# Attention of a four-stage kernel: two heads in one 32-row PSUM tile, earlier row turns, another order of the splits

## The reference

```python
q = q.reshape(B, S, H, DK); k = k.reshape(B, S, H, DK); v = v.reshape(B, S, H, DK)
scores = jnp.einsum('bqhd,bkhd->bhqk', q, k) / np.sqrt(DK)
attn = jax.nn.softmax(scores, axis=-1)
o = jnp.einsum('bhqk,bkhd->bqhd', attn, v).reshape(B, S, D)
x = x + o @ w_o + b_o            # layer 0; layer 1 multiplies by proj_w.T and adds proj_b
```

## Time and profile before

| what | value |
|---|---|
| median of 3 runs | 1201.21 us (1199.15 to 1223.79) |
| the profiled execution | 1201.9 us |
| its span | 1200.1 us |
| mean granted TensorE clock | 0.859 of 2.4 GHz |
| attention of layer 0, about | 92 to 359 us |
| attention of layer 1, about | 796 to 1031 us |
| PE, DVE, ACT, POOL busy | 70%, 69%, 51%, 39% of the span |

### The profile page before, as it was taken

One profiled execution on the slowest core, in us unless ns is written; L12 is line 12 of the kernel. 1 busy time (PEld: TensorE's weight loads), 2 busy tenths in 40 slices (PEclk: granted clock), 3 DMA queues, 4 the chain that ended last, 5 costly groups with the idle time before them and its releaser, 6 DMA issues. The chain is left out here.

```text
span 1200.1 us, 24485 instructions
## 1 busy us (share of the span) xinstructions
PE 839.7 (70%) x6994; PEld 483.7 (40%) x6994; DVE 824.7 (69%) x1748; ACT 610.8 (51%) x1269; POOL 465.8 (39%) x700
## 2 busy tenths in 40 slices
PE   2856888888862688878893444438999989567663
PEld 1631333333322466666682222213333333245443
DVE  5636888888828244555443688757888987399983
ACT  2752666666534155655462576616767777222221
POOL 3861233333330566767652344321111111155553
PEclk9985999999875699999897666758999999788896
DMA  6482222222100333433342143341212120000000
GB/s 208 141 272 76 61 63 63 63 63 63 50 14 1 99 120 106 126 107 118 114 124 76 52 140 108 117 143 47 65 55 67 55 67 28 1 10 9 17 18 17
DMA packets 111514, 94.28 MB, mean 79 GB/s; under 512 B 10671, under 2 KB 98506, under 8 KB 111328
## 3 DMA queue, kind: packets, MB, share of 16 engines
q1 hardware_dynamic: 105920, 83.31, 22.3%
q0 software_dynamic: 4608, 8.93, 2.5%
q10 hardware_dynamic: 928, 1.32, 0.3%
HBM read 59.18 MB, written 34.08 MB: 78 GB/s over the span
## 5 line engine op out<-in xcount | busy, mean ns | idle before, releaser
L973 DVE TENSOR_REDUCE neg_max<-bank 128x2 f32<-128x512 f32 x512 | 324.2, 684 | 55.0 <-PE bank L1083 54.5
L1063 ACT ACTIVATE pr<-score 128x512 f32<-128x512 f32 x512 | 280.0, 603 | 149.6 <-PE score L1140 147.5
L1140 PE MATMUL score<-qs,ks 51*128 51x256 bf16 x1024 | 177.7, 282 | 45.8 <-DMA qs<-max_rows 32.8
L1083 PE MATMUL bank<-ks,qs 48*128 48x256 bf16 x1024 | 182.5, 290 | 31.5 <-DMA qs<-q_scratch 30.8
L1158 PE MATMUL p_o<-pr,vs 128*9 128x256 f32 x2048 | 167.9, 395 | 0.4 <-ACT pr L1063 0.4
L1140 PEld LDWEIGHTS score<-qs,ks 51*128 51x128 bf16 x1024 | 68.0, 96 | 197.7 <-issue 72.2
L917 POOL TENSOR_TENSOR max_parts<-neg_max,one 128x16 bf16<-128x16 f32 x64 | 13.8, 216 | 266.0 <-DVE neg_max L973 266.0
L1322 POOL DMA_INDIRECT y_scratch<-y_all,to_i x72 | 76.6, 1064 | 67.0 <-DVE y_all L1428 57.6
L1316 POOL DMA_INDIRECT y_all<-hn_scratch,token_i x72 | 75.6, 1050 | 54.9 <-DVEq L1409 34.0
L1502 ACT ACTIVATE h_t<-p_t,vec 128x128 f32<-128x128 f32 x72 | 33.0, 458 | 120.6 <-PE p_t L1598 59.8
L1619 PE MATMUL p_y<-w,hid 128*128 x576 | 87.5, 297 | 0.1
(11 more groups left out here) (287 smaller groups left out, 1725.9 us busy)
## 6 DMA issues: line engine op xcount, KB each, us to landing
w_now<-w_dram SPq DMA_DIRECT2D x72, 256.0 KB
ks<-k_scratch SPq DMA_DIRECT2D x128, 96.0 KB, 2.2
qs<-q_scratch SPq DMA_DIRECT2D x128, 96.0 KB, 2.3
k_scratch<-parts SPq DMA_DIRECT2D x16, 384.0 KB, 2.6
q_scratch<-parts SPq DMA_DIRECT2D x16, 384.0 KB, 2.6
k_scratch<-parts SPq DMA_DIRECT2D x16, 256.0 KB, 2.2
q_scratch<-parts SPq DMA_DIRECT2D x16, 256.0 KB, 2.5
both<-y_scratch SPq DMA_DIRECT2D x8, 512.0 KB, 4.0
```

The lines of the kernel that those rows point to most:

```text
L973: dve.tensor_reduce(neg_max[:, i // HALF, :, col:col + 1], bk[:].rearrange("p (q t) -> p q t", t=L), AX.X, ALU.max, negate=True).then_inc( ...
L1063: act.activation(pr[s % N_PR][:, 2 * k:2 * k + 2, :], score[k][:], ACT.Exp, scale=SCALE).then_inc(exp_done, 1)
L1083: return pe.matmul(bk[:, qt * L:(qt + 1) * L], qs[u][rows, place(h), qt * P:(qt + 1) * P], ks[u][rows, place(h), :], start=True, stop=True)
L1140: scored = pe.matmul(score[k][:, j, :], ks[u][rows, place(h), kt * P:(kt + 1) * P], qs[u][rows, place(h), :], start=True, stop=True)
```

## The change

1. Two heads share a 32-row tile. The value operand `vs` has 18 columns for each head, 9 of them zero: heads of an even head group use columns 0 to 8, those of an odd group 9 to 17. The products of four steps (two head groups) are added up in the same PSUM rows. `p_o` has one 256-column region for each half of the heads. ScalarE moves 128 x 256 instead of 128 x 512, TensorE turns 4 blocks in all instead of 8, and one division (reciprocal of 128 x 32, product of 128 x 256) stands for two. The rows of the output weights are put in the new order on the host.
2. The uses: three "norm" uses (divide at step 2, turn at 3, project at 4) instead of four, and none at step 1; "rows" 0 goes ahead of the scores and maxima of step 5 instead of behind them.
3. GpSimd: `rows_ready(b - 2)` right after split half 1, instead of `rows_ready(b - 1)` after split half 0; `x_now`, `mv`, `ve` get two buffers for it; `copy_v` becomes two copies; two memsets of `vs` at the start of each attention. Its loop is written out. SP stores the rows of b - 2 behind the first of the two row transfers.
4. A sequence has 21 uses instead of 22, and TURN = 4 of them fill whole rounds of the banks: the middle 14 sequences are two written out and a loop over 3 x 4.

```diff
-        vs = [sb(f"vs{u}", [P, 2, H, VW]) for u in range(2)]
+        vs = [sb(f"vs{u}", [P, 2, H, 2 * VW]) for u in range(2)]
...
-        o_raw = sb("o_raw", [P, HG, L])
-        o_rec, o_n, o_t = sb("o_rec", [P, 2, H]), sb("o_n", [P, 2, H, DK]), sb("o_t", [P, L])
+        o_raw = sb("o_raw", [P, 2, L])
+        o_rec, o_n, o_t = sb("o_rec", [P, 2 * 2 * JT, 2]), sb("o_n", [P, 2 * 2 * JT, 2, DK]), sb("o_t", [P, L])
...
-        p_o = S.ps(ctx, "p_o", [P, HG, L])
+        p_o = S.ps(ctx, "p_o", [P, 2, 512])
...
-        AT = {1: [("rows", 1), ("norm", 0)], 2: [("norm", 1)], 3: [("norm", 2)], 4: [("norm", 3)], 5: [("rows", 0)]}
+        NORM = ("divide", "turn", "project")
+        AT = {1: [("rows", 1)], 2: [("norm", 0)], 3: [("norm", 1)], 4: [("norm", 2)]}
+        BEFORE = {5: [("rows", 0)]}
...
-            uses = [("max", head + 2), ("max", head)] + AT.get(s, [])
+            uses = BEFORE.get(s, []) + [("max", head + 2), ("max", head)] + AT.get(s, [])
...
-            if NB > 2:
-                with eng.Fori(0, (NB - 2) // 2) as pair:
-                    seq(pair * 2 + 1, 1, "middle")
-                    seq(pair * 2 + 2, 0, "middle")
-            seq(NB - 1, 1, "last")
+            ahead = (NB - 2) % TURN
+            for b in range(1, 1 + ahead):
+                seq(b, b % TURN, "middle")
+            with eng.Fori(0, (NB - 2) // TURN) as turn:
+                for b in range(1 + ahead, 1 + ahead + TURN):
+                    seq(turn * TURN + b, b % TURN, "middle")
+            seq(NB - 1, (NB - 1) % TURN, "last")
...
                 load(b + 2, u, 0)
                 maxima_to_queries(b + 1, 1 - u, 0, left(b, kind, ("rows", 0)))
+                if keeps:
+                    keep_rows(b - 2, u)
                 sp.wait_ge(score_full, (b + 1) * HALVES)
                 load(b + 2, u, 1)
                 maxima_to_queries(b + 1, 1 - u, 1, left(b + 1, "middle", ("rows", 1)))
-                if kind != "start":
-                    keep_rows(b - 1, 1 - u)
...
-                pool.tensor_copy(vs[u][:], S.v_all[:, bass.ds(2 * b, 2), :, :]).then_inc(v_copied, 1)
+                for a in range(2):
+                    held = vs[u][:].rearrange("p k (g a j) w -> p (k g) a j w", a=2, j=JT)[:, :, a, :, a * VW:(a + 1) * VW]
+                    whole = S.v_all[:, 2 * b:2 * b + 2, :, :].rearrange("p k (g a j) w -> p (k g) a j w", a=2, j=JT)
+                    copied = pool.tensor_copy(held, whole[:, :, a, :, :])
+                copied.then_inc(v_copied, 1)
...
+            for u in range(2):
+                pool.memset(vs[u][:], 0.0).then_inc(v_cleared, 1)
+            pool.wait_ge(v_cleared, 2)
...
-            if NB > 2:
-                with pool.Fori(0, (NB - 2) // 2) as pair:
-                    for u in range(2):
-                        b = pair * 2 + u + 1
-                        split(b, 1, left(b - 1, "middle", ("max", H - 3)))
-
-                        pool.wait_ge(pr_free, b * STEPS + N_PR)
-                        copy_v(b + 1, u)
-                        split(b + 1, 0, left(b, "middle", ("max", HALF - 3)))
-                        rows_ready(b - 1, u, pair)
+            for b in range(1, NB - 1):
+                split(b, 1, left(b - 1, "start" if b == 1 else "middle", ("max", H - 3)))
+                if b > 1:
+                    rows_ready(b - 2)
+
+                pool.wait_ge(pr_free, b * STEPS + N_PR)
+                copy_v(b + 1, (b + 1) % 2)
+                split(b + 1, 0, left(b, "middle", ("max", HALF - 3)))
...
-                    sn.turn((c * 2 + stage) * 1)
-                    heads = bk[:].rearrange("p (h r) -> p h r", r=32)
-                    sn.link(dve.reciprocal(o_rec[:, stage, :].unsqueeze(2), heads[:, :, DK:VW]))
-                    dve.tensor_tensor(o_n[:, stage], heads[:, :, 0:DK],
-                                      o_rec[:, stage, :].unsqueeze(2).broadcast_to([P, H, DK]), ALU.mult
-                                      ).then_inc(bank_free, 1)
...
+                    sn.turn(c)
+                    heads = bk[:].rearrange("p (t r) -> p t r", r=32)[:, :, 0:2 * VW].rearrange("p t (a w) -> p t a w", w=VW)
+                    sn.link(dve.reciprocal(o_rec[:], heads[:, :, :, DK]))
+                    dve.tensor_tensor(o_n[:], heads[:, :, :, 0:DK], o_rec[:].unsqueeze(3).broadcast_to([P, 2 * 2 * JT, 2, DK]),
+                                      ALU.mult).then_inc(bank_free, 1)
...
-                two = slice(2 * half, 2 * half + 2)
-                act.copy(o_raw[:, two, :], p_o[:, two, :]).then_inc(o_moved, 1)
...
+                act.copy(o_raw[:, half, :], p_o[:, half, 0:L]).then_inc(o_moved, 1)
...
-                    for hg in range(HG):
-                        last = pe.transpose(bk[:, hg * P:(hg + 1) * P], o_raw[:, hg, i * P:(i + 1) * P], S.ident)
...
+                    for qt in range(2):
+                        for half in range(2):
+                            at = (qt * 2 + half) * P
+                            last = pe.transpose(bk[:, at:at + P], o_raw[:, half, qt * P:(qt + 1) * P], S.ident)
...
-                    last = pe.matmul(p_o[32 * j:32 * j + VW, hg, :], vs[u][:, kt, hg * JT + j, :],
-                                     pr[s % N_PR][:, j, :], start=kt == 0, stop=kt == 1)
+                    last = pe.matmul(p_o[32 * j:32 * j + 2 * VW, hg // 2, 0:L], vs[u][:, kt, hg * JT + j, :],
+                                     pr[s % N_PR][:, j, :], start=s % (STEPS // 2) == 0,
+                                     stop=s % (STEPS // 2) == STEPS // 2 - 1)
```

More of the change, by code:

```diff
@@ L761, in phase_attention @@
         if layer == 0:
[L762 removed]
+            stats, rstd = sb("stats", [P, 2, 6]), sb("rstd", [P, 2])
+            mv, ve, x_now = ([sb(f"{n}{u}", [P] + shape) for u in range(2)]
+                             for n, shape in (("mv", [2, 2]), ("ve", [2]), ("x_now", [2, ROW])))
             hn = [sb(f"hn{u}", [P, 2, D]) for u in range(2)]
[L764 removed]
+            lg_raw = sb("lg_raw", [P, 2, E])
             stats_done, mv_done, var_ready, rstd_ready, hn_ready, lg_scaled = (
@@ L804, in base, with bank_of @@
             return 0 if kind == "first" else BASE0 if kind == "start" else BASE1 + (b - 1) * len(SEQ)
-        def bank_of(kind, u, i):
-            before = {"first": 0, "start": BASE0, "middle": BASE1 + (1 - u) * len(SEQ), "last": BASE1}[kind]
+        def bank_of(kind, v, i):
+            before = {"first": 0, "start": BASE0}.get(kind, BASE1 + (v - 1) % TURN * len(SEQ))
             return bank[(before + i) % N_BANK]
@@ L878, in follow @@
                 maxima_to_queries(b + 1, 1 - u, 1, left(b + 1, "middle", ("rows", 1)))
-                if kind != "start":
-                    keep_rows(b - 1, 1 - u)
             maxima_to_queries(0, 0, 0, left(0, "first", ("rows", 0)))
             maxima_to_queries(0, 0, 1, left(0, "start", ("rows", 1)))
[L884 to L888, removed]
-            follow(NB - 3, 1, "middle")
+            follow(0, 0, "start", False)
+            follow(1, 1, "middle", False)
+            with sp.Fori(0, (NB - 4) // 2) as pair:
+                follow(pair * 2 + 2, 0, "middle")
+                follow(pair * 2 + 3, 1, "middle")
             maxima_to_queries(NB - 1, 1, 0, left(NB - 2, "middle", ("rows", 0)))
-            keep_rows(NB - 3, 1)
+            keep_rows(NB - 4, 0)
             maxima_to_queries(NB - 1, 1, 1, left(NB - 1, "last", ("rows", 1)))
@@ L895, in _ @@
             if layer == 0:
+                keep_rows(NB - 3, 1)
                 keep_rows(NB - 2, 0)
@@ L1002, in norm @@
                         dve.wait_ge(hn_ready, c + 1)
-                        dve.tensor_tensor(x_now[:], S.rows[:, two, :], proj, ALU.add).then_inc(bank_free, 1)
+                        dve.tensor_tensor(x_now[u][:], S.rows[:, two, :], proj, ALU.add).then_inc(bank_free, 1)
                     else:
@@ L1006, in norm, with statistics @@
                                           ).then_inc(bank_free, 1)
-            def statistics(c, x_added):
+            def statistics(c, u, x_added):
                 dve.wait_ge(bank_free, x_added)
@@ L1012, in statistics, with variances @@
                 for n in range(2):
-                    last = dve.bn_stats(stats[:, n, :], x_now[:, n, 0:D])
+                    last = dve.bn_stats(stats[:, n, :], x_now[u][:, n, 0:D])
                 last.then_inc(stats_done, 1)
-            def variances(c):
+            def variances(c, u):
                 dve.wait_ge(stats_done, c + 1)
@@ L1037, in _ @@
             if layer == 0:
-                dve.sem_inc(hn_ready, 1)
+                dve.sem_inc(hn_ready, 2)
             for i, what in enumerate(FIRST):
-                consume(0, i, bank_of("first", 0, i), what)
+                consume(0, 0, i, bank_of("first", 0, i), what)
             sequences(dve, seq)
-            for stage in range(4):
+            for stage in range(len(NORM)):
                 i = len(LAST) + stage
```

(11 more changed lines are left out.)

93 lines of the change are left out of this document (50 added, 43 removed).

## The result

The changed kernel takes 1132.6 us (median of 4 runs, 1130.1 to 1135.9) beside 1201.7 before: a ratio of 0.943, 95% interval 0.940 to 0.947. The forecast was 1147 in a range of 1128 to 1174: direction and place were right, the gain was larger than forecast. The measured time is outside the 1140 to 1154 that the forecast itself covered.

The account below looks back on a forecast made before the run. VectorE was taken as nearly the bound, made to wait by in-order TensorE. Savings of 31.9 us (layer 0), 18.3 (layer 1) and 4.4 (edges), together 54.6 from 1201.9, gave 1147 us, range 1128 to 1174.

Parts of the forecast that it names:

- Step 1 and the transfer of half 1: Layer 1: step 2 starts 0.58 us earlier, but step 4 waits for half 1's rows until 6.2, losing 0.25.
- Rows 0 before step 5: Layer 1: SP starts half 0 about 0.85 us behind step 5 instead of 1.96; rows land at 11.9.
- The rest of layer 1: Step 5 to next step 0: sequence reaches 11.9 us, plus 0.2 for queueing, taken as 12.1 instead of 13.41.
- Layer 0: Middle sequences: VectorE floor 12.4 us, the 1.0 us split wait gone; 12.7 us taken instead of 14.98.
- Weight load: Value products: 9 more columns cost 0 to 8 ns a load, 0 to 0.5 us a sequence; taken as 0.
- The loop of four: Loop body of four sequences may not stay held on the chip: 0 to 60 us; taken as 0.
- The clock: Both layers: clock falls come where TensorE's two 1 us stalls lie together; none expected after, inside 14.98 - 12.7.
- the edges: First and last sequences and tails: 0.6, 0.7 and 0.9 us saved, each twice, 4.4 us together.
- VectorE at its floor with no queueing: Rival, both layers: sequences of 12.4 and 11.5 us, gain 67, so 1135 us; chance 0.17.
- The half gain through a new wait: Rival: single division or GpSimd's split at step 5 holds TensorE 0.5 us in 28 sequences, 1161 us; chance 0.23.
- the transfers exchanged: Rival: layer 1's transfer wait merely becomes half 1's, layer 0 gains only the split's wait, 1170 us; chance 0.11.
- the slower side: Rival: 18-column value products lose side-by-side running (1237 us at 0.35 a step), or the loop stalls each turn; chance 0.04.

Follow-up runs that it names:

- e3: Changed kernel with only rows 0 back behind the scores and maxima of step 5; 1131.2 us, 0.967 of the kernel before.
- e4: Changed kernel with only rows_ready back behind split half 0, now of sequence b - 1; 1135.5 us, 0.970 of the kernel before.
- e10: Changed kernel with the turn back at step 4 and the output-weight product at step 5, each one step later; 1146.9 us, 0.944 of the kernel before.
- e8: Changed kernel with the division done as two reciprocals and two products again, on the one bank; 1105.2 us, 0.937 of the kernel before.
- e5: Changed kernel with one more, unread VectorE copy of 128 x 256 in each sequence; 1099.7 us, 0.933 of the kernel before.
- e11: Changed kernel with the copy of the turned block on ScalarE and a one-column memset on VectorE instead; 1132.6 us, 0.932 of the kernel before.
- e6: Kernel before the change with one more, unread VectorE copy of 128 x 256 in each sequence; 1181.4 us, ratio 1.002.
- e1: Changed kernel with the old order of rows and splits, so only the packing is left; 1152.4 us, 0.986 of the kernel before.

## Why the prediction was right, and where its sizes were off

**What bounds the kernel.** Right: TensorE's two waits on the path of the maxima. e3 and e4 brought them back one at a time.

**Step 1 and the transfer of half 1.** The forecast was step 4 at 6.2 from zero, where the rows land, and so "late next". It came at 6.18, in a profile that lists no wait for it. That a gap of 0.07 us decides there showed only when e10 took the other path away.

**Rows 0 before step 5.** Right in kind: SP 0.71 us behind the step for 0.85 forecast, the wait gone, worth 0.75 and 1.21 us (e3). GpSimd's thin cover held; no wait for it at step 5.

**The rest of layer 1.** The chain gave 11.9, and 11.80 was measured. The step that was off is "I add 0.2 for queueing between the two and take 12.1": nothing came on top of the chain. 14 x 0.27 = 3.8 us.

**Layer 0.** The same: I took 12.7 over a floor of 12.4 and it came to 12.28, 14 x 0.42 = 5.9 us. The floor itself was too high. Busy time counts each instruction to the end of its record, and where VectorE runs without a break the next one starts some 0.08 us before that end (a reduction lasts 0.68 and the next follows after 0.60). Where TensorE was late before the change, this overlap was missing, and the time looked like work. The sum of starts, 12.31, is the right one. The split's wait left 0.3 us each of its 1.0.

**VectorE's division.** Forecast 0.64 from start to start; it is 865.93 - 865.20 = 0.73, because the reciprocal of 32 takes 342 ns and not about 300. Undone (e8) it is worth 7 us: it was priced as VectorE's work, but in layer 1 it counts through the turn that waits for it.

**ScalarE's move.** 378 ns for a forecast of 400.

**Weight load.** 96 ns instead of 89, so 7 ns for 9 columns, near the upper bound of 8; the nearest row, by which I took 0, was misleading. It is hidden all the same: the score follows the value products by 0.56 us (862.98 to 863.54), as the 0.56 of before in the earlier trace rows (937.01 to 937.57). The Trainium skill's rule on loads ("TensorE: Matmul & The Clock Gate", section "LDWEIGHTS (loading the stationary operand)") gave 7.5 ns for the difference, by an estimate, and the trace agrees for these two. The 13 us that it would have cost unhidden didn't come.

**The loop of four.** At nothing, and right for TensorE. The whole run has 40 instruction packets on one queue for 30 before. From 205 to 282 us, which takes in the loop's turn at about 243 us, the changed kernel shows none of them and one on the other queue:

```profile
q8 instruction: 40, 0.66, 0.2%
```

```profile
q1 hardware_dynamic: 12808, 6.05, 27.0%
q14 instruction: 1, 0.01, 0.0%
```

No packet comes on the first queue from 193 to 205 us either, where the loop turns for the first time. So the turns bring no burst of packets, and the body of four seems to be held as well. The Trainium skill's page "Runtime: NRT & Kernel Launch" (section "Instruction fetch mechanics") has it so for TensorE, with 2,048 instructions.

**The clock.** Right that the falls go with the two stalls: 1.00 in both layers. But the edges were sized from transposes and division alone, at 4.4 us; they came to 9, and 2 us more came from code that the change doesn't touch. The term that was mis-sized is "0.7 for a last sequence": that of layer 0 ran in part at 1.2 GHz before (0.77 from 333.8 to 348.9 us), which the earlier trace rows doesn't cover, and gained 4.1. A look at the clock of the edges, not of the middle alone, would have shown it. The prediction's premise, that each fall comes where two stalls of 1 us lie together, is too narrow: e4 has one stall a sequence and more falls.

**The rivals.** VectorE at its floor with no queueing, 1135, had 0.17 and is nearest to the measured 1131 of the profile, outside the forecast's own 1140 to 1154, though e5 and e11 show that VectorE's total isn't the reason. The half gain through a new wait, the transfers exchanged, and the slower side (columns, loop) didn't happen.

## What to carry to other kernels

The waits were found by reading each stage alone, and moving the order of two engines around one transfer was worth four times as much here as halving the data that is moved, turned and divided. When a wait is removed, write down the loop that closes next, from start to start, with transfers in it; it gives the period, and it says which work lies in the shadow of a transfer and is free. Relieving an engine that is busy 99% changed nothing where what was taken away lay in that shadow (e11), and moving the same work out of it cost its full length in layer 0 (e10).

## What the runs showed of the hardware

- VectorE was busy 163.34 of 165.62 us in layer 1 and still took 14 more copies of 284 ns at 0.3 us in all (e5). Records of neighbouring instructions overlap by some 0.08 us where it runs without a break (reductions of 0.68 us start 0.60 apart), so up to that much slack at each one reads as busy; starts are what to add up.
- The granted clock fell with TensorE's stalls, but not by a fixed rate. With two of 1.0 us in a sequence it was 0.95 (before) and 0.88 (e6, the same waits), with one of 2.1 it was 0.92 (e4). With one of 0.9 to 1.2 it was 0.98 (e1 and e3, layer 1), 0.99 (before, layer 1; e3, layer 0) and 1.00 (e6, layer 1). With one of 0.8 beside a shorter one (e10, layer 0) and with none over 0.3 (changed) it was 1.00.
- A pair of transfers of 6 KB, issued in 1.5 us, was used by the score 3.0 to 3.1 us behind SP's start where TensorE stood waiting for it (before, e1, e3, e10), and 2.95 behind it in the changed kernel, where the two arrive together.
- A weight load of 18 fp32 columns took 96 ns against 89 for 9 and 92 for 24 bf16 columns, with the pace of the four value products beside each other unchanged.
